# Where the three short parts of q and k are made: from ScalarE and VectorE to GpSimd

## The reference

```python
def proj(w, b):
    y = jnp.einsum('btd,ed->bte', x, w) + b
    return y.reshape(B, T, H, dk).transpose(0, 2, 1, 3)
q = proj(w_q, b_q)
k = proj(w_k, b_k)
v = proj(w_v, b_v)
scores = jnp.einsum('bhtd,bhsd->bhts', q, k) / jnp.sqrt(jnp.float32(dk))
attn = jax.nn.softmax(scores, axis=-1)
```

## Time and profile before

| | us |
|---|---|
| three runs | 539.05, 540.28, 540.39 (median 540.28) |
| the profiled execution: its own time | 542.95 |
| its span (first to last instruction) | 540.9 |
| busy PE / DVE / ACT / POOL | 484.6 / 398.8 / 359.0 / 170.8 |

### The profile page before, as it was taken

One profiled execution on the slowest core, in us unless ns is written; L12 is line 12 of the kernel. 1 busy time (PEld: TensorE's weight loads), 2 busy tenths in 40 slices (PEclk: granted clock), 3 DMA queues, 4 the chain that ended last, 5 costly groups with the idle time before them and its releaser, 6 DMA issues.

```text
span 540.9 us, 10853 instructions
## 1 busy us (share of the span) xinstructions
PE 484.6 (90%) x3376; PEld 270.5 (50%) x3376; DVE 398.8 (74%) x1072; ACT 359.0 (66%) x708; POOL 170.8 (32%) x500
## 2 busy tenths in 40 slices
PE   2457997989999999998899999999999999999993
PEld 1212443444444444444345665666656665666661
DVE  4678786879999989898725859587776859485453
ACT  2424786758888988888685566757756666755442
POOL 5054231323544435320002223515152533302020
PEclk9999999989999999999699999999999999999998
DMA  6334356333333333331014343535263544535321
GB/s 186 108 118 144 97 173 195 122 117 116 106 110 98 114 109 115 115 114 38 3 60 141 117 162 118 193 103 196 87 179 115 180 157 138 196 100 197 138 78 39
DMA packets 52456, 67.47 MB, mean 125 GB/s; under 512 B 5168, under 2 KB 36784, under 8 KB 52144
## 3 DMA queue, kind: packets, MB, share of 16 engines
q1 hardware_dynamic: 52400, 66.78, 39.2%
HBM read 51.17 MB, written 15.20 MB: 123 GB/s over the span
## 4 chain that ended last, share of the span: by engine, by line
PE 70%; DVE 7%; ACT 7%; SPq 5%; issue 5%; POOL 3%; DMA 2%; ACTq 0%; POOLq 0%; DVEq 0%
PE pY L1278 12%; PE pS L1278 12%; PE pO L1199 8%; PE pS L1264 6%; PE pS L1266 6%; PE pS L1265 6%; PE pS L1143 6%; PE pS L1149 3%; DVE mneg L859 3%; ACT probs L643 2%; SPq L387 2%; SPq L375 2%; PE pX L1128 2%; DMA k_scratch<-k_parts 2%; PE pX L1131 1%
## 5 line engine op out<-in xcount | busy, mean ns | idle before, releaser
L859 DVE TENSOR_REDUCE mneg<-pS 128x2 f32<-128x512 f32 x256 | 164.2, 686 | 31.8 <-PE pS L1143 31.0
L643 ACT ACTIVATE probs<-pS 128x512 f32<-128x512 f32 x256 | 143.9, 595 | 31.7 <-PE pS L1149 30.3
L718 ACT ACTIVATE h_ring<-r 128x512 f32<-128x512 f32 x144 | 90.4, 629 | 88.9 <-DVE r L1013 68.3
L1013 DVE SCALAR_TENSOR_TENSOR r<-pS,c_ring 128x512 f32<-128x512 f32 x128 | 87.6, 689 | 45.6 <-PE pS L1266 44.2
L1143 PE MATMUL pS<-kp,qp 48*128 48x256 bf16 x512 | 88.8, 295 | 24.9 <-DVE mneg L859 9.9
L1264 PE MATMUL pS<-qp,up_hi 128*128 128x512 f32 x144 | 103.5, 719 | 0.0
L1149 PE MATMUL pS<-qp,kp 51*128 51x256 bf16 x512 | 89.1, 287 | 0.8 <-ACT probs L643 0.5
L1199 PE MATMUL pO<-probs,vv 128*32 128x256 f32 x1024 | 76.6, 408 | 0.4 <-ACT oT_sb L594 0.4
L1278 PE MATMUL pS<-h_ring,down_sb 128*128 128x512 f32 x144 | 73.8, 594 | 0.0
L1278 PE MATMUL pY<-h_ring,down_sb 128*128 128x512 f32 x144 | 73.4, 595 | 0.0
L1143 PEld LDWEIGHTS pS<-kp,qp 48*128 48x128 bf16 x512 | 34.9, 97 | 75.3 <-DVE mneg L859 41.7
(11 more groups left out here) (178 smaller groups left out, 682.3 us busy)
## 6 DMA issues: line engine op xcount, KB each, us to landing
c_ring<-c_scratch SPq DMA_DIRECT2D x64, 512.0 KB, 3.9
qp<-q_scratch SPq DMA_DIRECT2D x64, 96.0 KB
kp<-k_scratch SPq DMA_DIRECT2D x64, 96.0 KB
q_scratch<-q_parts SPq DMA_DIRECT2D x16, 192.0 KB, 2.3
k_scratch<-k_parts SPq DMA_DIRECT2D x16, 192.0 KB, 2.4
q_scratch<-q_parts SPq DMA_DIRECT2D x16, 128.0 KB, 2.2
k_scratch<-k_parts SPq DMA_DIRECT2D x16, 128.0 KB, 2.2
out_x<-ot SPq DMA_DIRECT2D x7, 256.0 KB, 4.5
```

Source lines behind the costliest of these rows:

```text
L643: nc.scalar.activation(probs[j][:, hh], pS2[n % S2_RING][:, :, :], ACT.Exp, scale=SCALE).then_inc(exp_done, 1)
L718: nc.scalar.activation(h_sb[n % HRING], r_sb[n % URING][:, :], ACT.Square).then_inc(sq_done, 1)
L859: nc.vector.tensor_reduce(mneg[u % 2][:, :, hh, k], pS1[n % S1_RING][:, :].rearrange("p (a s) -> p a s", a=TH), AX.X, ALU.max, negate=True ...
L1013: nc.vector.scalar_tensor_tensor(out=r_sb[n % URING][:, :], in0=pU[n % URING], scalar=0.0, in1=c_ring[group % CRING][:, at], op0=ALU.max, ...
```

## The change

ScalarE no longer writes part 0 of q and k for projections 4 to 15: at the same two places it writes them in fp32 into new tiles `q_full` and `k_full`, which releases `pX` (`qk_taken`). GpSimd makes part 0 (two casts), the rests (two subtractions) and then parts 1 and 2 as before. VectorE's `rest` stays for batches 0 to 3 only.

```diff
+        q_full, k_full = sb("q_full", [P, T]), sb("k_full", [P, T])
...
             def part2(b):
-                pool.wait_ge(rest_done, b + 1)
+                pool.wait_ge(qk_taken, b + 1)
+                if b >= AHEAD:
+                    pool.wait_ge(scratch_done[b % 2], N_PARTS * (b // 2))
+                    nc.gpsimd.tensor_copy(q_parts[b % 2][:, 0], q_full[:, :])
+                    nc.gpsimd.tensor_copy(k_parts[b % 2][:, 0], k_full[:, :]).then_inc(part0_done, 1)
+                    pool.wait_ge(part0_done, b - AHEAD + 1)
+                    nc.gpsimd.tensor_tensor(q_rest[:, :], q_full[:, :], q_parts[b % 2][:, 0], ALU.subtract)
+                    nc.gpsimd.tensor_tensor(k_rest[:, :], k_full[:, :], k_parts[b % 2][:, 0],
+                                            ALU.subtract).then_inc(rests_done, 1)
+                    pool.wait_ge(rests_done, b - AHEAD + 1)
                 nc.gpsimd.tensor_copy(q_parts[b % 2][:, 1], q_rest[:, :])
                 nc.gpsimd.tensor_copy(k_parts[b % 2][:, 1], k_rest[:, :]).then_inc(part2_done, 1)
...
+            def full_q(b):
+                act.wait_ge(qk_done, b + 1)
+                act.wait_ge(part3_done, b)
+                nc.scalar.activation(q_full[:, :], pX[:, 0:T], ACT.Identity, bias=bqk_sb[:, 0:1])
+
+            def full_k(b):
+                nc.scalar.activation(k_full[:, :], pX[:, T:2 * T], ACT.Identity,
+                                     bias=bqk_sb[:, 1:2]).then_inc(qk_taken, 1)
...
                     if s == 0 and b >= 1 and b - 1 + AHEAD < NB:
-                        part1_k(b - 1 + AHEAD)
+                        full_k(b - 1 + AHEAD)
...
                     if s == 15 and proj:
-                        part1_q(b + AHEAD)
+                        full_q(b + AHEAD)
...
                     if u < NU:
                         row_max(u, s % 8 // 2, s % 2)
-                    if s == 2 and b >= 1 and b - 1 + AHEAD < NB:
-                        rest(b - 1 + AHEAD)
...
                         elif b - 1 + AHEAD < NB:
-                            pe.wait_ge(rest_done, b + AHEAD)
+                            pe.wait_ge(qk_taken, b + AHEAD)
```

More of the change, by code:

```diff
@@ L231, in block_kernel @@
         part1_done = sem("part1_done")
-        rest_done = sem("rest_done")
+        part0_done = sem("part0_done")
+        rests_done = sem("rests_done")
+        qk_taken = sem("qk_taken")
         part2_done = sem("part2_done")
@@ L609, in keep_xnT, with part1 @@
                 copy(xnT[b % 3][:, :], pX[:, 0:T]).then_inc(xnT_kept, 1)
-            def part1_q(b):
+            def full_q(b):
[5 more added lines that the diff above has]
+                                     bias=bqk_sb[:, 1:2]).then_inc(qk_taken, 1)
+            def part1(b):
                 act.wait_ge(qk_done, b + 1)
@@ L615, in part1_q @@
                 nc.scalar.activation(q_parts[b % 2][:, 0], pX[:, 0:T], ACT.Identity, bias=bqk_sb[:, 0:1])
-            def part1_k(b):
                 nc.scalar.activation(k_parts[b % 2][:, 0], pX[:, T:2 * T], ACT.Identity,
                                      bias=bqk_sb[:, 1:2]).then_inc(part1_done, 1)
-            def part1(b):
-                part1_q(b)
-                part1_k(b)
             def part2(b):
                 assert b < AHEAD
-                act.wait_ge(rest_done, b + 1)
+                act.wait_ge(qk_taken, b + 1)
                 copy(q_parts[b % 2][:, 1], q_rest[:, :])
@@ L841, in rest @@
                                                          op0=ALU.add, op1=ALU.subtract)
-                ins.then_inc(rest_done, 1)
+                ins.then_inc(qk_taken, 1)
             def keep_v(b):
@@ L1291, in project @@
                 if b >= 1:
-                    pe.wait_ge(rest_done, b)
+                    pe.wait_ge(qk_taken, b)
                 transpose_x(b)
@@ L1305, in _ @@
                     if u == 1 and k == 1:
-                        pe.wait_ge(rest_done, AHEAD - 1)
+                        pe.wait_ge(qk_taken, AHEAD - 1)
                         transpose_max(0)
@@ L1311, in _ @@
                     if u == 2 and k == 1:
-                        pe.wait_ge(rest_done, AHEAD)
+                        pe.wait_ge(qk_taken, AHEAD)
                         transpose_max(1)
```

## The result

| kernel | median us | runs | ratio to before, 95% interval |
|---|---|---|---|
| before | 540.39 | 9 (539.05 to 542.24) | |
| the change | 543.60 | 9 (541.66 to 546.06) | 1.0052 (1.0031 to 1.0073) |
| the change, a second time (c1) | 545.09 | 10, before at 541.48 | 1.0060 (1.0029 to 1.0091) |

What follows compares the result with a forecast made beforehand. The first half was taken as bound by the path ScalarE's k, VectorE's rests, GpSimd, TensorE. The terms 0.84 + 2.24 - 0.6 gave +2.5 us on 540.28, so 542.8 us, in a range of 539.4 to 546.0.

Steps and rivals of the forecast that it cites:

- The path: First half, project_k to transpose_x: ScalarE's k, GpSimd's block, xn, TensorE set its length; VectorE's 2.03 us leave it.
- The price: GpSimd's added block of two casts and two subtractions: 0.82 + 1.36 = 2.18 us.
- Ordinary projections: Projections 8, 10 and 13: GpSimd reaches the old casts, and xn follows, 0.21 us later each.
- Behind a chain: Projections 9, 11, 12 and 14, behind a layernorm chain: GpSimd's old casts 0.56 us later each, 2.24 in all.
- Projection 15: Makes no xn, but its parts are written later and TensorE waits for the DMA behind them: 0.21 us charged.
- The early projections: Projections 4 to 6 unchanged, bound by SP's queue and DMAs; projection 7 gains about 0.6 us.
- Faster: Rival: GpSimd gets through the new block in under 1.97 us, 2.3 us gained, 538.0 us; chance 0.12.
- No change: Rival: second halves shorten by the 0.2 to 0.6 us that first halves lengthen, 540.3 us; chance 0.21.
- Much slower: Rival: the new GpSimd subtractions take 0.85 us, twice VectorE's 0.42; 2.9 us on top, 545.7 us; chance 0.08.

Runs made afterwards that it cites:

- e1: The changed kernel with GpSimd's norm_x put ahead of its parts 0 to 2; 539.05 us, 0.9963 of the kernel before.
- e4: The changed kernel with one more GpSimd subtraction ahead of the two, in projections 4 to 15; 554.8 us against 541.6 before, ratio 1.0256.
- e5: The kernel before with VectorE's rests of projections 4 to 15 left out and nothing put in their place; 538.59 us against 541.48, ratio 0.9959.
- e8: The changed kernel with ScalarE's fp32 write of k put right behind that of q, ahead of the next batch's first exponential; 1.0025 of the kernel before.
- e6: The changed kernel with one more 512-column reduction from SBUF on VectorE in the first half, projections 4 to 15; 1.0052 of the kernel before.
- e7: The changed kernel with one more 512-column reduction from SBUF on VectorE in the second half; 548.39 us, 1.0141 of the kernel before.
- e3: The changed kernel with two operations like the old rests put back on VectorE at the same place, nobody waiting for them; 1.0104 of the kernel before.

## Why the prediction was right

**The path.** The mechanism was right, and is shown by e1, e4, e5 and e8: ScalarE's k, GpSimd's block, `xn`, TensorE. Shortening or lengthening a piece moved projection 8's half by that piece, down to the 6.05 us at which TensorE and its other waits take over.

**The price.** The block took 2.19 us for 2.18, the subtractions 0.67 for an fp32 output as for bf16. The factor of two for a two-input operation on GpSimd, in the Trainium skill's GPSIMD Engine Reference, section 4.1, does not hold at this size: 0.67 against 0.42 us.

**Ordinary projections.** 0.22 to 0.23 us each for 8, 10 and 13 in the profile, 0.21 forecast.

**Behind a chain.** 9, 11, 12 and 14: 0.75, 0.52, 0.51 and 0.30 us, 2.08 together, 2.24 forecast. The sum of the seven is 2.75 where the steps give 2.87. That the four agree so well is partly luck: the forecast took projection 11's rows for all of them, and 11 and 12 followed; in 9 the maxima ended later than in 11 (the first cast comes 2.00 us after `project_k` in place of 1.78), in 14 earlier (1.63), and the half was already 6.66 before.

**Projection 15.** 0.21 charged for the DMA behind it, 0 found: TensorE's wait for it is 0.31 us in place of 0.45, and the exponentials of batch 12 are 1.44 us late at its beginning and its middle.

**The early projections.** A gain of 0.6 forecast. In the profiled execution projection 7's half fell from 10.03 to 8.13 us while 6's grew by 0.56, and `project_k` of projection 8 ended 1.3 us earlier than before; in c1's only 0.4 earlier. This stretch differs from execution to execution (e6 and e7, with the change's block, have that end at 123.6 and 125.1 us), so one profile of each kernel neither shows the gain of 0.6 nor rules it out.

**What was not in the sum.** The clock near the end of the attention. The window of 252 to 290 us, before and after:

```profile
252.00:290.00 38.00, 33.69 (x311) 15.96 (x308) 20.05 (x75) 27.85 (x54) 3.44 (x13) 0.87 0.18 60
```

```profile
252.00:290.00 38.00, 33.79 (x309) 15.01 (x302) 19.18 (x70) 27.43 (x53) 2.79 (x9) 0.82 0.16 56
```

At the end of that window the changed kernel's lag has gone from 1.4 to 2.4 us, with the same instructions and a granted clock of 0.82 in place of 0.87. e6, the changed kernel with an idle reduction, has 0.96 there and a span of 539.8 us in its profile, though its median is the change's. So this share belongs to the execution, not shown to belong to the change, and a single profile's span says little about half a per cent.

The mean granted clock is known for every execution, and with it the part of the clock can be taken out. On c1's chip the kernel before ran from 538.5 us at 0.991 to 543.8 at 0.977, a wider spread than the whole change is worth. Executions with the same clock still differ by kernel: at 0.987 the change took 542.37, 542.54 and 543.91 us, before 539.35; at 0.977 546.48 against 542.83 to 543.84; at 0.939 545.05 against 541.88 and 545.03. A straight line through these 35 executions, over the time that each spent at the lower level, puts the change 2.7 us above before; this is an estimate from few executions. The seven halves give 2.75. The medians lie 0.5 to 0.6% up, 2.8 to 3.3 us. The forecast of 2.5 came as close as it did with a gain of 0.6 in it that is not shown and a 0.21 that was not there; without the two it would have been 2.9. Whether the longer waits of TensorE make low stretches of the clock likelier, as e4 suggests, stays open.

**The rivals.** Faster would have needed a block under 1.97 us: it was 2.19. No change would have needed shorter second halves: 8.31 after 8.32. Much slower would have needed a subtraction of 0.85: it was 0.67, but one of 0.85 is what e3 had by contention.

## What to carry to other kernels

Work should leave an engine in the stretch where that engine is the bound, and shouldn't land ahead of something that is waited for: read both from windows cut at the events of one loop, not from shares of the span. Here an engine with a third of its time in use was the wrong place, because its instructions run in order and the one TensorE waits for came last; putting that one first, two moved lines, gains 0.4 to 0.6% on either kernel's way of making the parts, and the freed VectorE adds nothing to it. Before moving work onto or beside GpSimd, look at what VectorE reads at that time.

## What the runs showed of the hardware

- GpSimd and VectorE slow each other: beside VectorE's operation with two SBUF inputs a GpSimd subtraction of 128x256 took 0.85 in place of 0.67 us and a cast up to 0.74 in place of 0.40; VectorE's own two took 1.55 for the pair, where the like operations of the kernel before took 0.47 each, and the cut's `tensor_scalar` with one SBUF input 0.87 in place of 0.42. Beside a reduction from SBUF or PSUM nothing changed (0.67).
- A wait of TensorE of 1.2 us was at times followed by a stretch at the lower of its two clock levels, which cost the second half 0.9 to 1.5 us; waits of 0.5 to 0.75 us in the profile of the change were not, in the stretch from 110 to 230 us. c1 had one such stretch, behind a wait of 0.76 us: batch 6's second half took 8.91 in place of 7.93.
